# Rope products of the next head pair: the shuffle moved into the even step and the sum ahead of the 256-key maximum, in a latent-attention and expert kernel

## What is computed

```python
norm_q = rmsnorm(x @ W_cq, q_scale)
q_nope = (norm_q @ W_dq_nope).reshape(B, S, NH, NOPE)
q_rope = apply_rope_single((norm_q @ W_dq_rope)..., cos, sin)
...
scores = einsum(query, key) * scale           # query = [q_nope, q_rope]
attn = softmax(where(causal, scores, -1e9))
out = einsum(attn, value)
```

## Time and profile before

| | value |
|---|---|
| median of three runs | 1363.62 us |
| profiled execution, its own time | 1362.68 us |
| its span in the trace | 1360.9 us |
| mean granted TensorE clock, share of full speed | 0.977 |
| TensorE busy over the span | 93% |
| VectorE, ScalarE, GpSimd busy | 62%, 60%, 44% |
| TensorE busy in 100 us of the first heads (300 to 400) | 99.81 us |
| TensorE busy in 100 us of the last heads (1100 to 1200) | 98.49 us |
| VectorE busy in the same two stretches | 76.92 and 79.72 us |

### The profile page before, as it was taken

One profiled execution on the slowest core, in us unless ns is written; L12 is line 12 of the kernel. 1 busy time (PEld: TensorE's weight loads), 2 busy tenths in 40 slices (PEclk: granted clock), 3 DMA queues, 4 the chain that ended last, 5 costly groups with the idle time before them and its releaser, 6 DMA issues. The chain is left out here.

```text
span 1360.9 us, 24106 instructions
## 1 busy us (share of the span) xinstructions
PE 1265.6 (93%) x7129; PEld 931.2 (68%) x7129; DVE 842.1 (62%) x3241; ACT 822.0 (60%) x2230; POOL 592.7 (44%) x510
## 2 busy tenths in 40 slices
PE   4999759999989999979999999998999999999996
PEld 3666536766757766657788888886566766666764
DVE  4577677777767777623333333333787788788783
ACT  1455427776666677635566666665676667677662
POOL 1111107676755676610000000000888888888860
PEclk8999979999999999989999999999999999999998
DMA  9977664343475443359976566664566676766651
GB/s 350 404 277 278 240 240 145 114 150 122 135 260 182 138 143 119 107 162 315 332 238 192 182 189 189 184 189 145 99 129 106 128 143 108 143 129 122 108 97 48
DMA packets 165970, 241.08 MB, mean 177 GB/s; under 512 B 24342, under 2 KB 138710, under 8 KB 160982
## 3 DMA queue, kind: packets, MB, share of 16 engines
q1 hardware_dynamic: 118038, 175.56, 38.8%
q0 software_dynamic: 36864, 53.50, 18.6%
q10 hardware_dynamic: 10944, 10.49, 2.7%
HBM read 122.05 MB, written 117.44 MB: 176 GB/s over the span
## 5 line engine op out<-in xcount | busy, mean ns | idle before, releaser
L1561 POOL DMA_INDIRECT l_sums<-sorted_y,slot_no x192 | 308.4, 1606 | 421.4 <-DMA l_sums<-base_dram 363.2
L1111 POOL DMA_INDIRECT sorted_x<-f_xn_row,slot_no x192 | 196.4, 1023 | 49.1 <-issue 44.4
L1246 ACT ACTIVATE f_prob<-f_prob,f_negmax 128x512 f32<-128x512 f32 (+3 forms) x256 | 142.3, 556 | 120.3 <-DVE f_negmax L1311 120.3
L1702 ACT ACTIVATE l_prob<-l_prob,l_negmax 128x512 f32<-128x512 f32 (+3 forms) x256 | 142.2, 556 | 118.9 <-DVE l_negmax L1768 118.9
L2088 DVE SCALAR_TENSOR_TENSOR act_f<-hidden,rows_in,ps 128x96 f32<-128x96 f32 x224 | 70.4, 314 | 230.5 <-ACT hidden L2051 230.3
L2013 PE MATMUL ps<-wgu_sb,xt_e 128*128 x896 | 184.2, 328 | 0.6 <-issue 0.5
L1159 PE MATMUL ps<-kt_s,f_qt 128*128 128x512 f32 (+3 forms) x512 | 171.0, 446 | 5.7 <-DVE f_qt L1302 4.4
L1601 PE MATMUL ps<-l_kt,l_qt 128*128 128x512 f32 (+3 forms) x512 | 170.0, 446 | 5.1 <-DVE l_qt L1759 4.5
L1311 DVE CUSTOM_DVE_ANT_0 f_prob<-ps,mask_add 128x512 f32<-128x512 f32 (+3 forms) x256 | 121.0, 486 | 75.4 <-issue 72.8
L1768 DVE CUSTOM_DVE_ANT_0 l_prob<-ps,mask_add 128x512 f32<-128x512 f32 (+3 forms) x256 | 121.1, 486 | 63.1 <-issue 61.6
L2013 PEld LDWEIGHTS ps<-wgu_sb,xt_e 128*128 128x128 f32 x896 | 139.9, 190 | 3.4 <-issue 2.6
(11 more groups left out here) (190 smaller groups left out, 2527.7 us busy)
## 6 DMA issues: line engine op xcount, KB each, us to landing
sorted_x<-zeros SPq DMA_DIRECT2D x14, 2304.0 KB, 10.3
rows_in<-sorted_x SPq DMA_DIRECT2D x112, 288.0 KB, 3.1
sorted_y<-rows_out SPq DMA_DIRECT2D x112, 256.0 KB, 2.1
f_norms<-norm_dram SPq DMA_DIRECT2D x64, 128.0 KB, 3.1
l_norms<-norm_dram SPq DMA_DIRECT2D x64, 128.0 KB, 3.4
wgu_sb<-in_wgu SPq DMA_DIRECT2D x16, 384.0 KB, 5.4
x_in<-in_x SPq DMA_DIRECT2D x8, 512.0 KB, 10.0
xn_dram<-xn SPq DMA_DIRECT2D x8, 512.0 KB, 4.6
```

The lines of the kernel that those rows point to most:

```text
L1111: pool.indirect_dma_start(sorted_x, bass.IndirectOffsetOnAxis(ap=slot_no[:, t, k:k + 1], axis=0), xn_row[buf][:], None).then_inc(scattered ...
L1246: act.activation(prob[:, i, qt, 0:w], prob[:, i, qt, 0:w], ACT.Exp, bias=negmax[:, i, qt:qt + 1], scale=-1.0, accum_out=rowsum[:, g // 2 % ...
L1561: pool.indirect_dma_start(sums[n % NSUM][:, t, :], None, sorted_y, bass.IndirectOffsetOnAxis(ap=slot_no[:, TT * GROUPS[n] + t, k:k + 1], a ...
L1702: act.activation(prob[:, i, qt, 0:w], prob[:, i, qt, 0:w], ACT.Exp, bias=negmax[:, i, qt:qt + 1], scale=-1.0, accum_out=rowsum[:, g // 2 % ...
```

## The change

Two moves on VectorE, the same in both heads parts. The rope shuffle of the next pair leaves the odd step and goes into the even step before it, between the maxima of blocks 2 and 3, with a wait for its own `q_turned`, so that the tile it writes has been read. In the odd step the even head's sum goes ahead of the maximum of block 2 (256 keys). In `between`, the odd head's sum goes behind the latent's normalisation and the inverses. No instruction is added or taken away; the other engines' code is unchanged.

```diff
-            def queries_rope(b, p):
-
+            def queries_swap(b, p):
+
+                if not (b == 0 and p == 0):
+                    dve.wait_ge(q_turned, NH * b + 2 * p)
                 dve.wait_ge(q_ready, 2 * (NP_ * b + p) + 2)
                 dve.stream_shuffle(qb[:], q_ps[1], SWAP)
+
+            def queries_rope(b, p):
+
                 dve.tensor_tensor(qa[:], q_ps[1], rope_t[:, 0, :], ALU.mult).then_inc(q_rope, 1)
...
             def between(bt, g):
 
                 p = g // 2
-                if g < NH:
-                    queries_sum(bt.now, p, 1)
                 if bt.back(g, 4):
                     b, h = bt.back(g, 4)
                     latent_norm(b, h // 2)
                 if bt.back(g, 2):
                     b, h = bt.back(g, 2)
                     inverses(b, h // 2)
+                if g < NH:
+                    queries_sum(bt.now, p, 1)
...
                 if nxt and par == 1:
                     queries_rope(*nxt)
+                if nxt and par == 1:
+                    queries_sum(*nxt, 0)
                 if now:
                     maxima(bt.now, g, 2)
-                if nxt and par == 1:
-                    queries_sum(*nxt, 0)
                 if par == 1 and bt.back(g, 5):
                     b, h = bt.back(g, 5)
                     latent_lo(b, h // 2)
+                if nxt and par == 0:
+                    queries_swap(*nxt)
                 if now:
                     maxima(bt.now, g, 3)
```

More of the change, by code:

```diff
@@ L1386, in _ @@
             dve.memset(rinv[:], 0.0)
+            queries_swap(0, 0)
             queries_rope(0, 0)
@@ L1853, in _ @@
             dve.wait_ge(last.loaded, 16 * last.LOADS)
+            queries_swap(HB, 0)
             queries_rope(HB, 0)
```

## The result

| | before | changed |
|---|---|---|
| median of the runs shown | 1363.67 us (4 runs, 1361.82 to 1365.32) | 1353.2 us (4 runs, 1352.11 to 1355.74) |
| ratio, 95% interval | | 0.9926 [0.9907, 0.9945] |
| profiled execution, its span | 1362.68 us, 1360.9 us | 1355.74 us, 1354.0 us |

The changed kernel is faster by 10.5 us of the median, where 14.5 us were forecast. Its median lies just inside the forecast's outer range (1346 to 1353.5 us) and outside that of the mechanism as described (1346.5 to 1350); two later repeats gave 1354.51 and 1353.98 us. Its profiled execution is the slowest of its four, so the two spans differ by less, 6.9 us.

What follows compares the result with a forecast made beforehand. Bound: TensorE's own work plus, once per pair, a sum or `lat_lo` that VectorE delivers late. 3.4 + 4.9 + 1.2 + 5.0 = 14.5 us off 1362.68 gives 1348.2 us; range 1346 to 1353.5.

Steps and rivals of the forecast that it cites:

- the mechanism as described: Both heads parts: block 0 and the pieces stop waiting for late VectorE results; 1348.2 us, range 1346.5 to 1350, chance 66%.
- start-up: Start of each heads part: the product's 1.52 us wait for the sum shortens by some 0.6 us, twice, 1.2 us.
- two changes of 0.31: First heads, odd-to-even changes: block 0's loss of 0.31 us behind the late sum goes, 15 times; 4.9 us with another.
- two of 0.21: Last heads, odd-to-even changes without a piece: block 0's mean loss of 0.21 us goes, 16 times, 3.4 us.
- one piece of 0.72: Last heads: output projection's piece gets `l_lat_lo` a sum earlier, winning 0.72 us, 7 times, 5.0 us.
- so all of the 0.72 us is won: Last heads' pieces: each waits 0.74 us for `l_lat_lo`, so the whole earlier arrival counts as gain.
- The first rival: First heads' odd steps: GpSimd comes before the sum, so block 0's loss falls by only some 0.1; 1351.2 us, 10%.
- "just" covered: First heads: `f_lat_lo` on GpSimd ends 0.2 us later, and its slack ahead of the pieces just covers that.
- The third rival: Even step: the shuffle does not fit and block 3's maximum is 0.62 us late; 1374 us, 4%.
- so the maximum of block 1 keeps its place: Even step, `between`: reordered operations last as before, so block 1's maximum does not move; cost nothing.
- going from 1010.43 to about 1011.5 costs nothing: Even step: the odd head's sum may come later, since the next step's block 0 reads it only at 1012.60.
- The second rival: Value products: new order in `between` costs 0.1 us at its joints, 34 pairs give back 3.4 us; 1351.6 us, 17%.

Runs made afterwards that it cites:

- e1: Changed kernel with the odd head's sum put back first in `between`, ahead of normalisation and inverses; 1349.41 us, repeat 1350.89 us.
- e4: Kernel before, with only the even head's sum moved ahead of block 2's maximum, shuffle left in the odd step; 1364.50 us, ratio 1.0005.
- e6: e1 with the shuffle ahead of block 2's maximum in the even step instead of behind it; 1376.29 us, ratio 1.0096.
- e7: e1 with a second shuffle of the same data into a spare tile right behind the first; 1372.02 us, ratio 1.0062.
- e3: Changed kernel with the odd head's sum between normalisation and inverses in `between`; 1349.09 us, repeat 1348.80 us.
- e8: e1 with one memset of 128x32, read by nobody, behind the inverses in `between`; 1349.61 us, ratio 0.9899.
- e5: Kernel before, with only the shuffle moved into the even step, both sums where they stood; 1360.43 us, ratio 0.9976.

## Why the prediction was right and where it was wrong

**Right: the mechanism of the gain.** The sum ended late once per pair, and now block 0 starts 0.11 us behind block 3's record and lasts 0.59 us. It does so in every change from an odd to an even step but the start-up. Most of the pieces' seven waits is gone.

**The sizes.** In e1, which has the gain without the late maximum, eight first heads win 0.62 us (48.01 to 47.39); forecast were two changes of 0.31. Eight last heads win 1.28 us where two of 0.21 and one piece of 0.72 make 1.14. The rest, 0.14 us, is the piece: the forecast took its wait from the idle time, 0.74 us, and "so all of the 0.72 us is won". By the starts it lost 0.99 us and more (1.02 to 1.07 against 0.03), of which 0.85 are won and 0.15 are left, since `l_lat_lo` is still its releaser. Over seven pieces this makes 1.0 us more than forecast. The start-up brought some 0.45 us each time and not 0.6.

**Right: GpSimd and the shuffle's place.** The first rival did not come: sum 442.74, GpSimd 442.95, a lead of 0.21 us where 0.2 was reckoned (443.50 against 443.68 in the time of the kernel before). e4 shows what the other order costs. That GpSimd's later end would be "just" covered had no number, and was luck: at the pieces whose `f_lat_lo` ends latest, it ended 0.31 us before the piece's first product and now ends 0.15 us before it, the distance at which the waiting pieces of the last heads start. The third rival did not come either: in e6 the same shuffle one maximum earlier costs 27 us, and e7 bears out the 0.08 us of slack that the forecast left behind block 3's maximum.

**Wrong: "each of the sum, the normalisation and the inverses takes as long as before ... so the maximum of block 1 keeps its place".** The operations do last as before. The joints between them do not: 0.07 us of overlap before the maximum became a distance of 0.14, and 0.09 us in all were left of this at the end of block 2's maximum, since the normalisation gained at its own joint. The Trainium skill (VectorE: DVE Perf Modes, "Two Vector instructions with no wait between them") tells of an instruction being held, until all earlier ones have finished, where an operand begins in another quadrant of partitions than that of the one before. The odd head's sum reads and writes partitions 64 to 127, the instructions around it begin at partition 0. The trace of e4 takes one part of this apart. There the even head's sum, which writes the same partitions but reads 0 to 63, stands directly ahead of block 2's maximum:

```profile
1051.50 0.69 DVE L1758 TENSOR_TENSOR l_qt<-l_qa,l_qb 64x512 f32<-64x512 f32 x1
1052.23 0.42 DVE L1767 CUSTOM_DVE_ANT_0 l_prob<-ps,mask_add 128x256 f32<-128x256 f32 x1
```

The maximum (of 256 keys here, of 384 in the changed kernel) starts 0.04 us behind the end of that sum, in all 62 places, and 0.14 us behind the odd head's sum in the changed kernel. So 0.10 us go with the partitions that the sum reads, which agrees with the Trainium skill; the other 0.11 us, from the transposition's 0.07 before its end to 0.04 behind the sum's, no run takes apart.

The second half of the same step was worse: "the sum made there is read by the next step's block 0 ... going from 1010.43 to about 1011.5 costs nothing". True of the sum. But block 0 of the odd step has a second condition, block 2's maximum of the even step, which sits behind `between` on the same engine. The earlier trace rows had both numbers: that maximum ends at 1012.35 and the product starts at 1012.60, and the runs put what it needs at 0.22 us, so 0.03 us were free and 0.09 came. I looked for the readers of the moved sum, and at the value products for the cover of a later block 1, and not at the reader of the next maximum. The second rival had the right cause and size (joints of 0.1 us, 34 pairs, 3.4 us; measured 0.09 and 2.5 us) and the wrong reader. The value products did not give way: their first one starts 0.42 us behind block 1's second in all 31 odd steps of each part, before and after. TensorE was itself some 0.07 us later by then, so this does not say how much room they had. "A transposition of order within `between` shifts nothing" was said of the steps with a piece, and there it held: the odd head's block 0 behind a piece keeps its record of 0.59 us.

**Not foreseen: the borders of the stages.** Over eight heads the changed kernel wins 0.49 us in the first heads and 1.10 in the last, so 8 x 1.59 = 12.7 us in the loops, were all their stretches alike. Apart from the start-up the forecast put everything outside them at nothing. The profiled spans differ by 6.9, so 5.8 us are lost outside the regular stretches. From the last piece of the first heads to the first product of the last heads it takes 358.7, 359.05 and 359.0 us in the three traces of the changed kernel, 356.6 before; 357.9 and 359.0 in e1, 357.6 and 356.5 in e3. A further 3 to 4 us lie at the batch border and at the start of both parts, where the step from head 0 to head 1 lasts 6.97 and 7.05 us and before 6.15 and 6.05. The granted clock goes with it: in the first 10 us of each part it is 0.73 and 0.72, before 0.81 and 0.83. The same where the first heads end, in windows from 575 to 610 us (length, busy us of PE, PEld, DVE, ACT and POOL with their counts, granted clock, DMA share, GB/s), first the kernel before:

```profile
575.00:610.00 35.00, 24.96 (x155) 19.90 (x152) 7.21 (x24) 11.38 (x30) 6.71 (x6) 0.90 0.45 137
```

then the changed kernel:

```profile
575.00:610.00 35.00, 24.66 (x140) 21.36 (x139) 7.00 (x23) 10.74 (x27) 5.64 (x6) 0.80 0.47 138
```

and e3:

```profile
575.00:610.00 35.00, 25.98 (x153) 20.97 (x154) 7.44 (x23) 11.23 (x32) 3.84 (x4) 0.90 0.58 178
```

The clock there is 0.80, 0.85 and 0.80 in the three traces of the changed kernel, 0.85 in both of e1, 0.90 in both of e3 and before. By the clock's records the whole profiled execution spends 64 us at the lower of its two levels (1.2 and 2.4 GHz) before, 72 to 75 in the changed kernel, 68 in e1 and 58 to 59 in e3. The trace that lost 5.8 us has 11 us more of it than the kernel before. An estimate from this: were TensorE the bound in all of these, half the clock would cost 5.6 us. But TensorE is not busy throughout there, the kernel before has one trace only, and no run changed the clock and nothing else, so this stays open. The latents' normalisation in the first heads waits for the norms' transfer once before and in e3 (7.0 and 7.6 us), and twice in the changed kernel and e1 (10.9 and 10.5). That the batch border is 1.2 us shorter in e3 than in e1 goes with it. The cause of either is open.

The sum by its own terms: 14.5 forecast, less 2.5 for the late maximum, less 0.3 for the start-up, plus 1.0 for the pieces, makes 12.7, the same as the loops give. The three jobs gave 10.5, 9.9 and 9.6 us, so 2 to 3 us are lost that these terms do not hold. They fit the borders above, which are known from profiled executions alone.

In short, two steps of the forecast failed. The new order in `between` was put at nothing, on the ground that block 1's maximum keeps its place, and it costs some 2.5 us. Everything outside the loops was left out, and it costs 2 to 3 us more, by a cause that is not shown. That 1353.2 still lies within the outer range is owed to the room made for the rivals, not to the mechanism as described.

## What to carry to other kernels

When instructions change places on an engine that runs without idle time, list the readers of everything that comes behind them up to the next idle stretch, not only the readers of what is moved: each is late by the change of the joints, and one of them may have no slack. Read an instruction's cost as the distance between starts in the very order in which it will stand; the drawn durations stay the same while the joint moves by 0.1 us, and once per pair that was a sixth of the forecast gain. Two executions of near twins also differ at the borders of the stages, here by some us; compare stretches inside the loop before you explain a difference of the totals. A change of two moves may hold one that brings nothing by itself: here the sum alone gave nothing and the shuffle alone 2.9 us, the two with the old order in `between` 13 to 15.

## What the runs showed of the hardware

- The joint ahead of a maximum: it starts 0.07 us before the end of a transposition, 0.04 us behind the end of a sum that reads partitions 0 to 63 and writes 64 to 127 (e4), and 0.14 us behind one that reads and writes 64 to 127 (changed kernel). A memset of 128x32, drawn 0.09 us long, moved the next instruction by 0.04 to 0.05 us (e8).
- A score product whose maximum ends less than 0.22 us ahead of its start has its record lengthened by what is missing: 0.595 us at a distance of 0.246, 0.612 at 0.202, 0.657 at 0.158, 0.667 at 0.147.
- VectorE's operations with two SBUF inputs and GpSimd's `f_lat_lo` take turns. GpSimd takes 1.27 us alone (e5), 1.55 where it starts 0.28 us behind VectorE's product, 1.61 to 1.65 where it starts 0.2 us behind the sum; in the last two it ends 1.13 to 1.14 us behind the end of VectorE's operation. A sum that starts 0.44 us into it took 1.65 us (e4), one that starts 1.29 us into it 0.80; both end 0.55 us behind GpSimd's end.
- A shuffle out of PSUM is drawn 0.73 us long and holds VectorE 0.62 to 0.64 us.
- The mean granted clock from 575 to 610 us was 0.80 to 0.85 in three traces of the changed kernel, 0.85 in two of e1 and 0.90 in two of e3, though all three do the same work.
